# Cross attention: queries and keys in high and low parts, both projections on four 64x64 squares

## The chip, the core and the metric

The kernel runs on one core of a Trainium2 chip. The metric is the device time of one execution in microseconds (us). TensorE (PE) multiplies matrices, VectorE (DVE) and ScalarE (ACT) do the element-wise work, GpSimd (POOL) small side jobs, SyncE (SP) issues the DMAs. A matrix product has a part that is held in TensorE's array (the weights, loaded first: "PEld" in the profile) and a part that streams through it. The results land in PSUM, eight banks of 128 partitions x 512 floats.

## The reference, cut to what matters

One decoder layer on x (32 sequences of 64 tokens, 512 features): a linear attention with 32 heads, a cross attention, and a product with a 512x512 matrix. Each adds to x and starts with a layer norm. The change is in the cross attention, in the way its queries and keys are made and multiplied:

```python
q = jnp.einsum('dc,bct->btd', Wq, init) + bq
k = jnp.einsum('dc,bct->bdt', Wk, init) + bk[None, :, None]
R = jnp.einsum('btd,bds->bts', q, k)
attention = jax.nn.softmax(R, axis=-1)
v = jnp.einsum('oc,bct->bto', Wv, x) + bv
out = jnp.einsum('bts,bsc->bct', attention, v)
```

`init` is the context: 64 channels by 512 positions for each of 32 sequences. Wq and Wk are 64x64, so each sequence has a 64x512 query, a 64x512 key and 512x512 scores.

## The kernel before, in words

`attention` does the linear attention and is not touched. `cross_and_ffn` does the rest for pairs of sequences, t = 0 to 15; sequence 2t lies on partitions 0 to 63, sequence 2t+1 on 64 to 127. All engines run programs written out by hand, in order, joined by semaphores. Work on pair t is interleaved with the scores of pair t+1, the projections of pair t+2 and the last product (`ffn`) of pair t-1.

One pass of TensorE's loop over t is, in this order: `turn(t,0)` (8 transposes of probabilities), `project_q(t+2)`, `turn(t,1)`, `project_k(t+2)`, the scores of column blocks 0 and 1 of pair t+1, `spread_scale(t)`, `weigh(t,0)` and `weigh(t,1)` (probabilities times values), `turn(t,2)`, `values(t+1)`, the scores of blocks 2 and 3, `turn_xn3(t-1)`, `turn(t,3)`, `weigh(t,2)`, `weigh(t,3)`, `ffn(t-1)`. Passes 14 and 15 have no projection.

- `project_q` and `project_k` (L1177 to 1184) multiply 128 partitions of context by a 128x128 matrix that holds the 64x64 weight twice on its diagonal and zeros elsewhere. The operands are plain float32, and the trace has two matmul records for each such product.
- `cross_scores` (L1186 to 1193) takes one 64-row product for each sequence, held on rows 0 to 63 and 64 to 127 of the array, also in plain float32: two records each.
- ScalarE copies the projections out of PSUM with the bias (`keep_q`, `keep_k`). Both use bank 7 (MISC), one after the other; `spread_scale` and `values` use the same bank later.
- VectorE takes the maximum of each row of scores (`row_max`), ScalarE the exponentials (`exps`). Scores of blocks 0 and 2 go to banks 0 and 1, those of 1 and 3 to banks 2 and 3, so scores of block 3 wait for both exponentials of block 1.
- `ffn` already works with high and low parts: operands of type float32r, three products, one record each (L1249 to 1251).

Ahead of the loop, pair 0 is projected, scored and exponentiated, pair 1 projected, and the first two layer norms, `values(0)` and the high and low parts of the 512x512 matrix (`eye_hi`, `eye_lo`) are made.

Of the kernel before, what the change touches and what calls it, by code (L numbers as in the profile page):

```python
# [14 lines left out]
ACT = mybir.ActivationFunctionType  # L15
# [4 lines left out]
P = 128  # L20
# [27 lines left out]
class Prepared:  # L48


    def __init__(self, sb, sem, ctx_in, consts):
        self.ctx_in = ctx_in
        self.consts = consts
        self.ctx = sb("ctx", [P, 2, D])
        self.wq = sb("wq2", [P, P])
        self.wk = sb("wk2", [P, P])
        self.wv = sb("wv2", [P, P])
        self.bias = sb("bias2", [P, 3])
        self.ms = sb("ms", [P, TILES])
        self.ctx_landed = [sem(f"ctx_landed{i}") for i in range(2)]  # L60
        self.consts_landed = sem("consts_landed")
        self.summed = sem("summed")
        self.ms_ready = sem("ms_ready")
# [23 lines left out]

def load_ctx(sp, pre, t):
    sp.dma_start(pre.ctx[:, t % 2], pre.ctx_in[t]).then_inc(pre.ctx_landed[t % 2], 16)


def attention(nc, sb, sem, bank, attn_acc, sq_acc, ident, ones, pre, x, w_pairs, w_v, w_out, norm_w, decay, ident_in):
# [811 lines left out]
def cross_and_ffn(nc, sb, sem, bank, x1, ident, pre, x, eye_in, out):  # L904
    with ExitStack() as own:
        xr = sb(own, "xr", [P, TILES, D])
        rrms = sb(own, "rrms", [P, TILES])
        minus_half = sb(own, "minus_half2", [P, TILES])
        q = sb(own, "q", [P, 2, D])
        k = sb(own, "k", [P, 2, D])  # L910
        minus_max = sb(own, "minus_max", [P, 2, CH, 2])
        row_sum = sb(own, "row_sum", [P, 2, CH, 2])
        row_inv = sb(own, "row_inv", [P, 2, CH, 2])
# [14 lines left out]
        shift = sb(own, "shift", [P, 2])  # L928

        names = """rrms_ready x1_ready eye_landed consts_set eye_hi_cut eye_cut  # L930
            qk_mm qk_ready s_mm max_ready exp_ready inv_ready turned probT_a_ready probT_b_ready
            v_mm v_ready scale_mm scale_ready pv_mm scaled x2_ready
            ln2_stats ln2_var ln2_eps ln2_root ln2_rstd xn2_ready
            ln3_stats ln3_var ln3_eps ln3_root ln3_rstd xn3_ready
# [3 lines left out]
        x_t = x.rearrange("b s d -> (b s) d").rearrange("(k t p) d -> k p t d", t=TT, p=P)  # L938
        out_t = out.rearrange("b s d -> (b s) d").rearrange("(t p) d -> t p d", p=P)
        PAIRS = TILES  # L940
        PT, OUT, MISC = 4, 6, 7

        with nc.Block() as block:

            @block.sync
            def _(sp):
                def load_x(n):
                    sp.dma_start(xr[:, n * TT:(n + 1) * TT], x_t[n]).then_inc(x_back[n], 16)

                load_x(0)  # L950
                sp.dma_start(eye[:, :, :], eye_in).then_inc(S["eye_landed"], 16)
                for n in range(1, TB):
                    load_x(n)
                for t in range(PAIRS):
                    if t + 2 < PAIRS:
                        sp.wait_ge(S["qk_mm"], 2 * t + 2)
                        load_ctx(sp, pre, t + 2)
                    if t >= 2:
                        sp.wait_ge(S["out_ready"], t - 1)
                        sp.dma_start(out_t[t - 2], x1[:, t - 2]).then_inc(S["stored"], 16)  # L960
                for t in range(PAIRS - 2, PAIRS):
                    sp.wait_ge(S["out_ready"], t + 1)
                    sp.dma_start(out_t[t], x1[:, t]).then_inc(S["stored"], 16)
                sp.wait_ge(S["stored"], 16 * PAIRS)
# [28 lines left out]

            @block.scalar
            def _(act):
                def keep_q(t, at):
                    act.wait_ge(S["qk_mm"], 2 * t + 1)
                    nc.scalar.activation(q[:, t % 2], bank[:, at], ACT.Identity,
                                         bias=pre.bias[:, 0:1]).then_inc(S["qk_ready"], 1)

                def keep_k(t, at):
                    act.wait_ge(S["qk_mm"], 2 * t + 2)
                    nc.scalar.activation(k[:, t % 2], bank[:, at], ACT.Identity,
                                         bias=pre.bias[:, 1:2]).then_inc(S["qk_ready"], 1)

                def exps(t, j, i, at):
                    act.wait_ge(S["max_ready"], t * CH + (j + 1))
# [19 lines left out]
                    nc.scalar.activation(xn3_hi[:, :, :], bank[:, MISC].rearrange("p (c n) -> p c n", c=CH),  # L1027
                                         ACT.Copy).then_inc(S["xn3_hi_ready"], 1)

                keep_q(0, 6)  # L1030
                keep_k(0, 7)
                for j in range(CH):
                    for i in range(2):
                        exps(0, j, i, 2 * (j % 2))
                keep_q(1, 4)
                keep_k(1, 5)
                normed(2, 0, 0, xn2)
                act.wait_ge(S["v_mm"], 1)
                normed(2, 0, 1, xn2)
# [3 lines left out]
                for t in range(PAIRS):  # L1043
                    keep_turned(t, 0)
                    if t + 2 < PAIRS:
                        keep_q(t + 2, MISC)
                    keep_turned(t, 1)
                    if t + 2 < PAIRS:
                        keep_k(t + 2, MISC)
                    if t:  # L1050
                        normed(3, 1, t - 1, xn3)
                    if t + 1 < PAIRS:
                        exps(t + 1, 0, 0, 0)
                    keep_scale(t)
                    if t + 1 < PAIRS:
                        exps(t + 1, 0, 1, 0)
                        exps(t + 1, 1, 0, 2)
                    keep_turned(t, 2)
                    if t + 1 < PAIRS:
                        exps(t + 1, 1, 1, 2)  # L1060
                        exps(t + 1, 2, 0, 0)
                    if t:
                        xn3_high(t - 1)
                    keep_turned(t, 3)
                    if t + 1 < PAIRS:
                        exps(t + 1, 2, 1, 0)
                    if t + 1 < PAIRS:
                        exps(t + 1, 3, 0, 2)
                        exps(t + 1, 3, 1, 2)
                    if t + 2 < PAIRS:  # L1070
                        act.wait_ge(S["v_mm"], t + 2)
                        normed(2, 0, t + 2, xn2)
# [4 lines left out]
            def _(dve):  # L1077
                def row_max(t, j, at):
                    dve.wait_ge(S["s_mm"], t * CH + (j + 1))
                    nc.vector.tensor_reduce(minus_max[:, t % 2, j], bank[:, at:at + 2], AX.X, ALU.max,  # L1080
                                            negate=True).then_inc(S["max_ready"], 1)

                def inverse(t):
                    dve.wait_ge(S["exp_ready"], 2 * CH * (t + 1))
# [39 lines left out]
                def add_ffn(t):  # L1124
                    dve.wait_ge(S["ffn_mm"], t + 1)
                    nc.vector.tensor_tensor(x1[:, t], x1[:, t], bank[:, MISC], ALU.add).then_inc(S["out_ready"], 1)

                for j in range(CH):
                    row_max(0, j, 2 * (j % 2))
                dve.wait_ge(S["rrms_ready"], 1)  # L1130
                dve.wait_ge(x_back[0], 16)
                make_x1(0)
# [9 lines left out]
                                            ALU.subtract).then_inc(S["eye_cut"], 1)  # L1142
                for t in range(PAIRS):
                    keep_turned(t, 0)
                    keep_turned(t, 1)
                    if t + 1 < PAIRS:
                        row_max(t + 1, 0, 0)
# [26 lines left out]

            @block.tensor
            def _(pe):
                def project_q(t, at):  # L1177
                    pe.wait_ge(pre.ctx_landed[t % 2], 16 * (t // 2 + 1))
                    nc.tensor.matmul(bank[:, at], pre.wq[:, :], pre.ctx[:, t % 2], start=True, stop=True)\  # L1179
                        .then_inc(S["qk_mm"], 1)  # L1180

                def project_k(t, at):
                    nc.tensor.matmul(bank[:, at], pre.wk[:, :], pre.ctx[:, t % 2], start=True, stop=True)\  # L1183
                        .then_inc(S["qk_mm"], 1)

                def cross_scores(t, j, at):  # L1186
                    if j == 0:
                        pe.wait_ge(S["qk_ready"], 2 * t + 2)
                    for i in range(2):
                        s = slice(i * SEQ, (i + 1) * SEQ)  # L1190
                        m = nc.tensor.matmul(bank[:, at + i], q[s, t % 2, j * P:(j + 1) * P], k[s, t % 2],  # L1191
                                             start=True, stop=True)
                    m.then_inc(S["s_mm"], 1)

                def turn(t, c):
# [57 lines left out]
                    m.then_inc(S["ffn_mm"], 1)  # L1253

                pe.wait_ge(pre.consts_landed, 16 * 6)
                project_q(0, 6)
                project_k(0, 7)
                for j in range(CH):
                    if j == 2:
                        project_q(1, 4)  # L1260
                        project_k(1, 5)
                    if j >= 2:
                        pe.wait_ge(S["exp_ready"], 2 * (j - 1))
                    cross_scores(0, j, 2 * (j % 2))
                values(0)
                pe.wait_ge(S["qk_ready"], 4)
                pe.wait_ge(S["v_ready"], 1)
                for t in range(PAIRS):
                    turn(t, 0)
                    if t + 2 < PAIRS:  # L1270
                        if t >= 2:
                            pe.wait_ge(S["out_ready"], t - 1)
                        project_q(t + 2, MISC)
                    turn(t, 1)
                    if t + 2 < PAIRS:
                        pe.wait_ge(S["qk_ready"], 2 * t + 5)
                        project_k(t + 2, MISC)
                    if t + 1 < PAIRS:
                        cross_scores(t + 1, 0, 0)
                        cross_scores(t + 1, 1, 2)  # L1280
                    if t + 2 < PAIRS:
                        pe.wait_ge(S["qk_ready"], 2 * t + 6)
                    elif t >= 2:
                        pe.wait_ge(S["out_ready"], t - 1)
                    spread_scale(t)
# [74 lines left out]
```

## Time and profile before

| | us |
|---|---|
| three timed runs: median (lowest, highest) | 2226.3 (2224.16, 2227.65) |
| the profiled execution | 2226.27 |
| its span, first to last instruction | 2224.5 |
| PE busy, DVE busy, ACT busy | 2174.7, 1415.3, 1060.0 |
| linear attention, up to | 1896.5 |
| cross attention and last product | 328.0 |
| one pass of the loop over t | 18.68 |

Times in the rows below are microseconds from the start of the span. A timeline row has start, duration, engine, line, operation, output<-inputs, shapes and how many such instructions ran one after the other; in brackets stands how long the engine sat idle before and what ended that. A PE row's duration reaches to the modelled end of its last product, which overlaps the start of the next: the time that a group costs TensorE is the distance from its start to the start of the next group. On the array, "128*128" is the whole of it, "64*128" two halves by rows, "128*64" two halves by columns.

### The profile page before, as it was taken

The numbers are of one execution on the slowest core, as the hardware profiler recorded it, in microseconds if no ns is written. First come the engines' busy times: TensorE is split into PE (matmuls) and PEld (weight loads), VectorE is DVE, ScalarE is ACT, GpSimd is POOL, SyncE is SP. The second block draws the span as 40 slices with busy tenths as digits, with TensorE's granted clock in tenths as the row PEclk, the third lists the DMA queues.
The fourth block names the chain that finished last, engine by engine and source line by source line (L and its number), as shares of the span: only waits on it lengthen the run. The fifth ranks groups of instructions, "written<-read, shape, count | busy, mean of one in ns | idle before, by whom it ended". The sixth has DMA issues, their size and how long they took to land. (4 is left out here: it accounts for less than half of the span.)

```text
span 2224.5 us, 37071 instructions
## 1 busy us (share of the span) xinstructions
PE 2174.7 (98%) x13600; PEld 1793.2 (81%) x13600; DVE 1415.3 (64%) x1925; ACT 1060.0 (48%) x1799; POOL 651.9 (29%) x723
## 2 busy tenths in 40 slices
PE   6999999999999999999999999999999999799998
PEld 6888888888888888878888888888888888455555
DVE  6666666666666666676666666666666665577775
ACT  4444444444444444444444444444444443566664
POOL 5333333333333332343322333333333331111110
PEclk9999999999999999999999999999999999899999
DMA  3111111111111111111111111111111110200000
GB/s 128 57 49 41 47 40 48 48 48 48 48 48 48 48 40 47 50 39 41 48 48 48 48 48 48 48 40 46 41 48 48 48 49 23 110 29 29 29 24 20
DMA packets 37915, 104.91 MB, mean 47 GB/s; under 512 B 4448, under 2 KB 9056, under 8 KB 37728
## 3 DMA queue, kind: packets, MB, share of 16 engines
q1 hardware_dynamic: 37856, 104.10, 14.4%
q8 instruction: 39, 0.64, 0.1%
q14 instruction: 20, 0.16, 0.0%
HBM read 99.89 MB, written 4.19 MB: 47 GB/s over the span
## 5 line engine op out<-in xcount | busy, mean ns | idle before, releaser
L733 PE MATMUL bank<-x_hi,w_hi 128*128 128x512 f32 x1344 | 531.4, 395 | 2.4 <-ACT gate L384 2.4
L736 PE MATMUL bank<-x_hi,w_lo 128*128 128x512 f32 x1344 | 524.2, 390 | 1.2 <-issue 1.2
L735 PE MATMUL bank<-x_lo,w_hi 128*128 128x512 f32 x1344 | 523.1, 389 | 0.0
L733 PEld LDWEIGHTS bank<-x_hi,w_hi 128*128 128x128 f32 x1344 | 252.2, 188 | 59.3 <-ACT gate L384 3.3
L736 PEld LDWEIGHTS bank<-x_hi,w_lo 128*128 128x128 f32 x1344 | 252.3, 188 | 54.1
L735 PEld LDWEIGHTS bank<-x_lo,w_hi 128*128 128x128 f32 x1344 | 252.5, 188 | 50.8
L748 PE MATMUL bank<-wv_hi,x_hi 128*128 128x256 f32 x1024 | 293.1, 286 | 0.0
L306 POOL TENSOR_TENSOR sq_acc<-sq_acc,sq 128x512 f32<-128x512 f32 x124 | 160.5, 1295 | 445.7 <-ACT sq L434 432.5
L749 PE MATMUL bank<-wv_lo,x_hi 128*128 128x256 f32 x1024 | 290.4, 284 | 0.0
L750 PE MATMUL bank<-wv_hi,x_lo 128*128 128x256 f32 x1024 | 290.3, 283 | 0.0
L295 POOL TENSOR_TENSOR qk<-qk,sq 128x512 f32<-128x512 f32 x64 | 83.0, 1296 | 701.0 <-ACT sq L397 701.0
L506 DVE TENSOR_TENSOR w_lo<-raw,w_hi 128x1024 fp32r<-128x1024 f32 x192 | 239.5, 1249 | 8.8 <-ACT w_hi L349 8.8
L384 ACT ACTIVATE qk<-bank 128x512 f32<-128x512 f32 x192 | 115.2, 600 | 246.9 <-PE bank L736 246.6
L591 DVE TENSOR_TENSOR attn_acc<-attn_acc,bank 128x512 f32<-128x512 f32 x240 | 161.8, 685 | 69.9 <-PE bank L778 67.9
L776 PE MATMUL bank<-wo_hi,y_hi 128*128 128x512 f32 x512 | 203.3, 397 | 2.1 <-DVE y_lo L582 2.1
L778 PE MATMUL bank<-wo_hi,y_lo 128*128 128x512 f32 x512 | 202.6, 396 | 0.0
L777 PE MATMUL bank<-wo_lo,y_hi 128*128 128x512 f32 x512 | 202.5, 396 | 0.0
L349 ACT ACTIVATE w_hi<-raw 128x1024 fp32r<-128x1024 f32 x192 | 171.7, 945 | 57.5 <-POOL raw L282 57.5
L748 PEld LDWEIGHTS bank<-wv_hi,x_hi 128*128 128x128 f32 x1024 | 197.3, 193 | 1.2
L749 PEld LDWEIGHTS bank<-wv_lo,x_hi 128*128 128x128 f32 x1024 | 197.2, 193 | 1.2
L750 PEld LDWEIGHTS bank<-wv_hi,x_lo 128*128 128x128 f32 x1024 | 197.1, 193 | 0.0
L544 DVE TENSOR_TENSOR qk<-bank,qk 128x512 f32<-128x512 f32 x192 | 127.1, 689 | 85.2 <-ACT qk L399 42.7
(124 smaller groups left out, 3442.9 us busy)
## 6 DMA issues: line engine op xcount, KB each, us to landing
raw<-w_pairs SPq DMA_DIRECT2D x96, 512.0 KB, 3.4
raw<-w_v SPq DMA_DIRECT2D x32, 512.0 KB, 3.4
raw<-w_out SPq DMA_DIRECT2D x32, 512.0 KB, 3.3
ctx<-ctx_in SPq DMA_DIRECT2D x16, 256.0 KB, 2.8
xr<-x SPq DMA_DIRECT2D x4, 1024.0 KB, 10.9
out<-attn_acc SPq DMA_DIRECT2D x16, 256.0 KB, 2.0
attn_acc<-x SPq DMA_DIRECT2D x8, 256.0 KB, 6.5
decays<-decay SPq DMA_DIRECT2D x32, 64.0 KB, 1.9
```

The source lines that it names most:

```text
L349: nc.scalar.activation(dst[:, s], raw[:, s], ACT.Copy).then_inc(done, 1)
L506: nc.vector.tensor_tensor(dst[:, s], raw[:, s], hi[:, s].bitcast(F32), ALU.subtract).then_inc(done, 1)
L591: nc.vector.tensor_tensor(acc, acc, bank[:, out_bank(half, g, i)], ALU.add).then_inc(out_added, 1)
L733: nc.tensor.matmul(bank[:, to], w_hi[:, a, s], x_hi[:, b, c], start=part in ("first", "only") and c == 0, stop=False, skip_group_check=True)
L735: nc.tensor.matmul(bank[:, to], w_hi[:, a, s], x_lo[:, b, c], start=False, stop=False, skip_group_check=True)
L736: i = nc.tensor.matmul(bank[:, to], w_lo[:, a, s], x_hi[:, b, c], start=False, stop=part in ("last", "only") and c == 1, skip_group_check= ...
L748: nc.tensor.matmul(dst, x_hi[:, b, c % 2, s], wv_hi[:, m], start=(c == 0), stop=False)
L749: nc.tensor.matmul(dst, x_hi[:, b, c % 2, s], wv_lo[:, m], start=False, stop=False)
L750: k = nc.tensor.matmul(dst, x_lo[:, b, c % 2, s], wv_hi[:, m], start=False, stop=(c == CH - 1))
L776: nc.tensor.matmul(dst, y_hi[:, h, s], wo_hi[:, h], start=(h == 0), stop=False)
L777: nc.tensor.matmul(dst, y_hi[:, h, s], wo_lo[:, h], start=False, stop=False)
L778: k = nc.tensor.matmul(dst, y_lo[:, h, s], wo_hi[:, h], start=False, stop=(h == HG - 1))
```

## The change

Queries and keys are kept as two float32r numbers each, a high part (ScalarE's rounding copy) and a low part (what remains, a new operation of VectorE that reads PSUM and the high part). The scores are then the sum of three products, high x high, low x high and high x low, each on the same two 64-row halves of the array. Both projections of a pair are made by one function, as four 64x64 products, one in each quarter of the array: queries of the two sequences on the diagonal, keys on the other two. For the keys to land on the right partitions the context is also loaded with its halves swapped (`crossed`, two more DMAs for each pair). The second projection no longer has a place of its own in the loop; the keys get bank 3 (KEYS), which scores of block 1 need too, so these wait for the low part of the keys.

```diff
@@ load_ctx
     sp.dma_start(pre.ctx[:, t % 2], pre.ctx_in[t]).then_inc(pre.ctx_landed[t % 2], 16)
+    for i in range(2):
+        to, source = slice(i * SEQ, (i + 1) * SEQ), slice((1 - i) * SEQ, (2 - i) * SEQ)
+        sp.dma_start(pre.crossed[to, t % 2], pre.ctx_in[t, source]).then_inc(pre.ctx_landed[t % 2], 16)
@@ ScalarE
-                    nc.scalar.activation(k[:, t % 2], bank[:, at], ACT.Identity,
-                                         bias=pre.bias[:, 1:2]).then_inc(S["qk_ready"], 1)
+                def k_high(t, at):
+                    act.wait_ge(S["qk_mm"], t + 1)
+                    nc.scalar.activation(k_hi[:, t % 2], bank[:, at], ACT.Identity,
+                                         bias=pre.bias[:, 1:2]).then_inc(S["k_hi_ready"], 1)
                     keep_turned(t, 0)
                     if t + 2 < PAIRS:
-                        keep_q(t + 2, MISC)
+                        k_high(t + 2, KEYS)
+                        q_high(t + 2, MISC)
                     keep_turned(t, 1)
-                    if t + 2 < PAIRS:
-                        keep_k(t + 2, MISC)
@@ VectorE
+                def k_low(t, at):
+                    dve.wait_ge(S["k_hi_ready"], t + 1)
+                    nc.vector.scalar_tensor_tensor(out=k_lo[:, t % 2], in0=bank[:, at], scalar=pre.bias[:, 1:2],
+                                                   in1=k_hi[:, t % 2].bitcast(F32), op0=ALU.add, op1=ALU.subtract)\
+                        .then_inc(S["k_ready"], 1)
+                k_low(0, 7)
+                q_low(0, 6)
                 for j in range(CH):
                     row_max(0, j, 2 * (j % 2))
+                k_low(1, 5)
+                q_low(1, 4)
                 dve.wait_ge(S["rrms_ready"], 1)
                 dve.wait_ge(x_back[0], 16)
                 make_x1(0)
...
                     keep_turned(t, 0)
+                    if t + 2 < PAIRS:
+                        k_low(t + 2, KEYS)
+                        q_low(t + 2, MISC)
                     keep_turned(t, 1)
@@ TensorE
+                def project_qk(t, at_q, at_k):
+                    pe.wait_ge(pre.ctx_landed[t % 2], 48 * (t // 2 + 1))
+                    for r in range(2):
+                        rows, other = slice(r * SEQ, (r + 1) * SEQ), slice((1 - r) * SEQ, (2 - r) * SEQ)
+                        nc.tensor.matmul(bank[rows, at_q], pre.wq[rows, rows], pre.ctx[rows, t % 2], start=True, stop=True)
+                        m = nc.tensor.matmul(bank[other, at_k], pre.wk[rows, rows], pre.crossed[rows, t % 2],
+                                             start=True, stop=True)
+                    m.then_inc(S["qk_mm"], 1)
...
-                    for i in range(2):
-                        s = slice(i * SEQ, (i + 1) * SEQ)
-                        m = nc.tensor.matmul(bank[:, at + i], q[s, t % 2, j * P:(j + 1) * P], k[s, t % 2],
-                                             start=True, stop=True)
+                    for n, (a, b) in enumerate(((q_hi, k_hi), (q_lo, k_hi), (q_hi, k_lo))):
+                        for i in range(2):
+                            s = slice(i * SEQ, (i + 1) * SEQ)
+                            m = nc.tensor.matmul(bank[:, at + i], a[s, t % 2, j * P:(j + 1) * P], b[s, t % 2],
+                                                 start=(n == 0), stop=(n == 2))
...
                     turn(t, 0)
                     if t + 2 < PAIRS:
                         if t >= 2:
                             pe.wait_ge(S["out_ready"], t - 1)
-                        project_q(t + 2, MISC)
+                        project_qk(t + 2, MISC, KEYS)
                     turn(t, 1)
-                    if t + 2 < PAIRS:
-                        pe.wait_ge(S["qk_ready"], 2 * t + 5)
-                        project_k(t + 2, MISC)
                     if t + 1 < PAIRS:
                         cross_scores(t + 1, 0, 0)
+                        if t + 2 < PAIRS:
+                            pe.wait_ge(S["k_ready"], t + 3)
                         cross_scores(t + 1, 1, 2)
                     if t + 2 < PAIRS:
-                        pe.wait_ge(S["qk_ready"], 2 * t + 6)
+                        pe.wait_ge(S["q_ready"], t + 3)
```

`q_high` and `q_low` are the same for the queries.

How this moves TensorE's instructions, in the loop from one `ffn` to `values`. Before (L1203 is `turn`, L1179 and L1183 the projections, L1191 the scores, L1232 `spread_scale`, L1216 `weigh`, L1225 `values`):

```order
L1251 MATMUL bank<-eye_hi,xn_lo 128x512
L1203 MATMUL bank<-ident,prob 128x128 x8
L1179 MATMUL bank<-ctx,wq 128x512
L1203 MATMUL bank<-ident,prob 128x128 x8
L1183 MATMUL bank<-ctx,wk 128x512
L1191 MATMUL bank<-k,q 128x512 x4
L1232 MATMUL bank<-ident,row_inv 64x128 x8
L1216 MATMUL bank<-probT,v 64x512 x4
L1203 MATMUL bank<-ident,prob 128x128 x8
L1225 MATMUL bank<-wv,xn 128x128 x4
```

The same place in the changed kernel (L1230 is `turn`, L1206 and L1207 the squares, L1218 the scores, L1259 `spread_scale`):

```order
L1230 MATMUL bank<-ident,prob 128x128 x8
L1206 MATMUL bank<-ctx,wq 64x512
L1207 MATMUL bank<-crossed,wk 64x512
L1206 MATMUL bank<-ctx,wq 64x512
L1207 MATMUL bank<-crossed,wk 64x512
L1230 MATMUL bank<-ident,prob 128x128 x8
L1218 MATMUL bank<-k_hi,q_hi 128x512 x2
L1218 MATMUL bank<-k_hi,q_lo 128x512 x2
L1218 MATMUL bank<-k_lo,q_hi 128x512 x2
L1218 MATMUL bank<-k_hi,q_hi 128x512 x2
L1218 MATMUL bank<-k_hi,q_lo 128x512 x2
L1218 MATMUL bank<-k_lo,q_hi 128x512 x2
```

The key projection has moved from behind the second `turn` to the side of the query projection, and two blocks of scores are twelve products where they were four.

VectorE in the loop, from `add_ffn` to the first layer norm, before (L1126 is `add_ffn`, L1089 the copies of `turn`, L1080 `row_max`, L1092 `make_x1`):

```order
L1126 TENSOR_TENSOR attn_acc<-attn_acc,bank 128x512
L1089 COPY probT<-bank 128x512 x2
L1080 TENSOR_REDUCE minus_max<-bank 128x2 x2
L1092 SCALAR_TENSOR_TENSOR attn_acc<-attn_acc,rrms,xr 128x512
L1098 BN_STATS stats<-attn_acc 128x6
```

And in the changed kernel:

```order
L1143 TENSOR_TENSOR attn_acc<-attn_acc,bank 128x512
L1106 COPY probT<-bank 128x512
L1096 SCALAR_TENSOR_TENSOR k_lo<-bank,bias,k_hi 128x512
L1090 SCALAR_TENSOR_TENSOR q_lo<-bank,bias,q_hi 128x512
L1106 COPY probT<-bank 128x512
L1085 TENSOR_REDUCE minus_max<-bank 128x2 x2
L1109 SCALAR_TENSOR_TENSOR attn_acc<-attn_acc,rrms,xr 128x512
L1115 BN_STATS stats<-attn_acc 128x6
```

The two new operations stand between the copies of `turn(t,0)` and `turn(t,1)`, and so ahead of the maxima that the exponentials of pair t+1 wait for.

## Rows read from the trace of the kernel before

**Rows 1.** Windows: us, PE, PEld, DVE, ACT, POOL busy (instructions), PEclk, DMA share, GB/s
```profile
1910.80:1924.40 13.60, 8.50 (x28) 5.98 (x28) 5.36 (x9) 5.71 (x10) 1.94 (x6) 0.50 0.15 59
1924.40:2180.00 255.60, 254.06 (x1476) 145.87 (x1475) 182.17 (x259) 160.44 (x359) 28.37 (x81) 1.00 0.08 26
```
**Rows 2.** Timeline of PE, one pass of the loop (t = 9)
```profile
2087.24 1.03 PE L1203 MATMUL bank<-ident,prob 128*128 128x128 f32 x8
2088.18 1.13 PE L1179 MATMUL bank<-ctx,wq 128*128 128x512 f32 x2
...
2090.09 1.12 PE L1183 MATMUL bank<-ctx,wk 128*128 128x512 f32 x2
2091.14 1.99 PE L1191 MATMUL bank<-k,q 64*128 64x512 f32 x8
2093.06 1.09 PE L1232 MATMUL bank<-ident,row_inv 128*64 128x128 f32 x16
2093.98 1.89 PE L1216 MATMUL bank<-probT,v 128*64 128x512 f32 x8
...
2097.72 1.99 PE L1191 MATMUL bank<-k,q 64*128 64x512 f32 x8
...
2103.85 0.40 PE L1249 MATMUL bank<-eye_hi,xn_hi 128*128 128x512 f32 x1
2104.08 0.39 PE L1250 MATMUL bank<-eye_lo,xn_hi 128*128 128x512 f32 x1
...
2105.92 1.03 PE L1203 MATMUL bank<-ident,prob 128*128 128x128 f32 x8
```
**Rows 3.** Timeline of PEld, same pass: loads of the first scores and weights
```profile
2091.14 0.30 PEld L1191 LDWEIGHTS bank<-k,q 64*128 64x128 f32 x4 [0.76 <-issue]
...
2093.88 0.25 PEld L1216 LDWEIGHTS bank<-probT,v 128*64 128x64 f32 x4
```
**Rows 4.** Timeline of PE, pass 14, which has no projection
```profile
2182.56 1.07 PE L1203 MATMUL bank<-ident,prob 128*128 128x128 f32 x8 [0.87 <-DVE probT L1089]
2183.55 0.70 PE L1191 MATMUL bank<-k,q 64*128 64x512 f32 x2
```
**Rows 5.** Timeline of ACT, pass t = 9
```profile
2089.35 0.69 ACT L998 ACTIVATE q<-bank,bias 128x512 f32<-128x512 f32 x1 [0.43 <-PE bank L1179]
...
2093.58 0.69 ACT L1008 ACTIVATE prob<-bank,minus_max 128x512 f32<-128x512 f32 x1 [0.94 <-DVE minus_max L1080]
...
2095.97 0.22 ACT L1008 ACTIVATION_READ_ACCUMULATOR prob<-bank,minus_max 128x1 f32 x1
2096.93 0.60 ACT L1014 ACTIVATE probT<-bank 128x512 f32<-128x512 f32 x1 [0.75 <-PE bank L1203]
2097.42 0.68 ACT L1008 ACTIVATE prob<-bank,minus_max 128x512 f32<-128x512 f32 x1
2097.99 0.20 ACT L1008 ACTIVATION_READ_ACCUMULATOR prob<-bank,minus_max 128x1 f32 x1
```
**Rows 6.** Timeline of DVE, same pass
```profile
2088.31 0.69 DVE L1089 COPY probT<-bank 128x512 f32<-128x512 f32 x1 [0.19 <-PE bank L1203]
...
2092.32 2.35 DVE L1080 TENSOR_REDUCE minus_max<-bank 128x2 f32<-128x1024 f32 x2 [1.37 <-PE bank L1191]
```
**Rows 7.** Timeline ahead of the loop and in its pass 0, ACT
```profile
1910.35 0.69 ACT L1003 ACTIVATE k<-bank,bias 128x512 f32<-128x512 f32 x1
...
1917.71 2.19 ACT L1042 ACTIVATE eye_hi<-eye 128x512 fp32r<-128x512 f32 x4 [1.75 <-issue]
```
**Rows 8.** The same stretch, DVE
```profile
1908.32 0.74 DVE L1092 SCALAR_TENSOR_TENSOR attn_acc<-attn_acc,rrms,xr 128x512 f32<-128x512 f32 x1
```
**Rows 9.** The same stretch, PE
```profile
1921.62 1.94 PE L1203 MATMUL bank<-ident,prob 128*128 128x128 f32 x8 [2.30 <-DVE probT L1089]
1923.35 1.56 PE L1183 MATMUL bank<-ctx,wk 128*128 128x512 f32 x2
1924.84 1.99 PE L1191 MATMUL bank<-k,q 64*128 64x512 f32 x8
```

More of the change, by code:

```diff
@@ L54, in __init__ @@
         self.ctx = sb("ctx", [P, 2, D])
+        self.crossed = sb("crossed", [P, 2, D])
         self.wq = sb("wq2", [P, P])
@@ L908, in cross_and_ffn @@
         minus_half = sb(own, "minus_half2", [P, TILES])
-        q = sb(own, "q", [P, 2, D])
-        k = sb(own, "k", [P, 2, D])
+        q_hi = sb(own, "q_hi", [P, 2, D], F32R)
+        q_lo = sb(own, "q_lo", [P, 2, D], F32R)
+        k_hi = sb(own, "k_hi", [P, 2, D], F32R)
+        k_lo = sb(own, "k_lo", [P, 2, D], F32R)
         minus_max = sb(own, "minus_max", [P, 2, CH, 2])
@@ L930, in cross_and_ffn @@
         names = """rrms_ready x1_ready eye_landed consts_set eye_hi_cut eye_cut
-            qk_mm qk_ready s_mm max_ready exp_ready inv_ready turned probT_a_ready probT_b_ready
+            qk_mm q_hi_ready k_hi_ready q_ready k_ready s_mm max_ready exp_ready inv_ready turned probT_a_ready probT_b_ready
             v_mm v_ready scale_mm scale_ready pv_mm scaled x2_ready
@@ L940, in cross_and_ffn @@
         PAIRS = TILES
-        PT, OUT, MISC = 4, 6, 7
+        KEYS, PT, OUT, MISC = 3, 4, 6, 7
         with nc.Block() as block:
@@ L955, in _ @@
                     if t + 2 < PAIRS:
-                        sp.wait_ge(S["qk_mm"], 2 * t + 2)
+                        sp.wait_ge(S["qk_mm"], t + 1)
                         load_ctx(sp, pre, t + 2)
@@ L995, in _, with q_high @@
             def _(act):
[L996 to L1002, printed above, removed]
-                    nc.scalar.activation(k[:, t % 2], bank[:, at], ACT.Identity,
-                                         bias=pre.bias[:, 1:2]).then_inc(S["qk_ready"], 1)
+                def q_high(t, at):
+                    act.wait_ge(S["qk_mm"], t + 1)
+                    nc.scalar.activation(q_hi[:, t % 2], bank[:, at], ACT.Identity,
+                                         bias=pre.bias[:, 0:1]).then_inc(S["q_hi_ready"], 1)
+                def k_high(t, at):
+                    act.wait_ge(S["qk_mm"], t + 1)
+                    nc.scalar.activation(k_hi[:, t % 2], bank[:, at], ACT.Identity,
+                                         bias=pre.bias[:, 1:2]).then_inc(S["k_hi_ready"], 1)
                 def exps(t, j, i, at):
@@ L1028, in xn3_high @@
                                          ACT.Copy).then_inc(S["xn3_hi_ready"], 1)
-                keep_q(0, 6)
-                keep_k(0, 7)
+                k_high(0, 7)
+                q_high(0, 6)
                 for j in range(CH):
@@ L1034, in _ @@
                         exps(0, j, i, 2 * (j % 2))
-                keep_q(1, 4)
-                keep_k(1, 5)
+                k_high(1, 5)
+                q_high(1, 4)
                 normed(2, 0, 0, xn2)
@@ L1081, in row_max, with q_low @@
                                             negate=True).then_inc(S["max_ready"], 1)
+                def q_low(t, at):
+                    dve.wait_ge(S["q_hi_ready"], t + 1)
+                    nc.vector.scalar_tensor_tensor(out=q_lo[:, t % 2], in0=bank[:, at], scalar=pre.bias[:, 0:1],
+                                                   in1=q_hi[:, t % 2].bitcast(F32), op0=ALU.add, op1=ALU.subtract)\
+                        .then_inc(S["q_ready"], 1)
+                def k_low(t, at):
[3 more added lines that the diff above has]
+                        .then_inc(S["k_ready"], 1)
                 def inverse(t):
@@ L1176, in _ @@
             def _(pe):
[L1177 to L1184, printed above, removed]
+                def project_qk(t, at_q, at_k):
[6 more added lines that the diff above has]
+                    m.then_inc(S["qk_mm"], 1)
                 def cross_scores(t, j, at):
                     if j == 0:
-                        pe.wait_ge(S["qk_ready"], 2 * t + 2)
-                    for i in range(2):
-                        s = slice(i * SEQ, (i + 1) * SEQ)
-                        m = nc.tensor.matmul(bank[:, at + i], q[s, t % 2, j * P:(j + 1) * P], k[s, t % 2],
-                                             start=True, stop=True)
+                        pe.wait_ge(S["q_ready"], t + 1)
+                        pe.wait_ge(S["k_ready"], t + 1)
+                    for n, (a, b) in enumerate(((q_hi, k_hi), (q_lo, k_hi), (q_hi, k_lo))):
[3 more added lines that the diff above has]
+                                                 start=(n == 0), stop=(n == 2))
                     m.then_inc(S["s_mm"], 1)
@@ L1255, in _ @@
                 pe.wait_ge(pre.consts_landed, 16 * 6)
-                project_q(0, 6)
-                project_k(0, 7)
+                project_qk(0, 6, 7)
                 for j in range(CH):
                     if j == 2:
-                        project_q(1, 4)
-                        project_k(1, 5)
+                        project_qk(1, 4, 5)
                     if j >= 2:
@@ L1265, in _ @@
                 values(0)
-                pe.wait_ge(S["qk_ready"], 4)
+                pe.wait_ge(S["q_ready"], 2)
+                pe.wait_ge(S["k_ready"], 2)
                 pe.wait_ge(S["v_ready"], 1)
```

## The prediction

> **What bounds the kernel now.** I read the windows first, then the timelines of one pass of the loop over t, then the stretch ahead of the loop. The change leaves all up to 1896.5 us alone, so it can only act on the 328 us behind. From 1924.4 to 2180.0 PE is busy 254.1 of 255.6 us at a granted clock of 1.00, DVE 182.2, ACT 160.4 [rows 1]. A busy PE is not yet a PE that nothing holds up, so the timeline has to say it: in the pass from 2087.24 to 2105.92 (18.68 us) each group starts before the modelled end of the one before it [rows 2]. So TensorE's order sets the pass, and what leaves its order counts in full until something else is late. DVE works some 13.3 of the 18.68 us of a pass (182.2 of 255.6), ACT 11.7; they have room, but not at any moment.
>
> Ahead of the loop it is otherwise: TensorE waits 2.30 us for DVE at 1921.62 [rows 9], and from 1910.8 to 1924.4 the granted clock is 0.50, that is 1.2 GHz, with PE busy in 8.5 of 13.6 us [rows 1].
>
> **The change part by part.** The sum is made against the profiled execution, 2226.27 us (span 2224.5 and 1.8 around it); the median shown is 2226.3, the same for this purpose. I count times in a pass from its first row, 2087.24.
>
> *Projections.* From `project_q` at 2088.18 to the scores at 2091.14 lie 2.96 us: query projection, `turn(t,1)`, key projection [rows 2]. Afterwards there is one slot of squares and `turn(t,1)`. Pass 14, without projection, shows `turn(t,1)` directly ahead of the scores: 0.99 from start to start [rows 4]. For the slot of the squares I take 1.05, what `project_k` costs when the array's division changes behind it [rows 2]: all four squares stream 512 columns twice, as it does, if they run side by side. 2.96 - 1.05 - 0.99 = 0.92 saved in a pass. That they run side by side is the first thing no row shows. Nearest are `weigh`, two products in column halves that share all rows: 8 records end within 1.89 us and the first four weight loads take 0.25 [rows 2, 3], so they run in twos at 0.43 each (8 single ones at 0.43 would take 3.4); and the scores, two in row halves: 8 records in 1.92 [rows 2]. Squares are both at once. Bounds: four at once, and two at once, 0.86 more. I take four, since both halvings work.
>
> *Scores.* Two blocks cost 1.92 now: 8 records in twos, 4 x 0.43, and 0.20 of change of division. A block is 0.86. Products of float32r operands start 0.23 apart in `ffn` (2103.85 to 2104.08) [rows 2]. Three passes in twos: 0.69 a block, 0.17 less, four blocks 0.68 in a pass. Their weight loads: four 64-row loads fit in 0.30, in twos [rows 3], and one pair is needed every 0.23. Bounds: 0.43 / 2 for each pair, 0.65 a block, and, if these products don't run in twos, 6 x 0.23 = 1.38.
>
> *VectorE.* `k_low` and `q_low` are scalar_tensor_tensor of 128x512; this operation takes 0.74 on SBUF [rows 8]. Bounds 0.69 (a copy out of PSUM) and 1.22 (one `row_max` over twice the elements; two take 2.35) [rows 6]. I take 0.74, the nearest in kind. 13.3 + 1.5 = 14.8 us of a pass of over 17: no bound by volume. But they stand ahead of the maxima, so the chain behind them is to be walked. Squares start at 0.94; their copy starts 1.17 later as `q`'s does [rows 5], 2.11; `k_high` 0.69, 2.80; `k_low` to 3.57; `q_high` is ready by 3.5, `q_low` to 4.31; the copy of `turn(t,1)` to 5.00; first maximum 1.22, 6.22; first exponential at 6.26. Before it was at 2093.58, 6.34. So the two operations fit into the 1.37 us for which DVE waits now, nearly to the last tenth [rows 6]. The waits for `k_low` ahead of block 1 (3.57, PE comes there at 3.0 + 0.7 = 3.7) and for `q_low` ahead of `spread_scale` (4.31, PE comes at 4.6) cost nothing.
>
> *The wait that appears.* Scores of block 3 need both exponentials of block 1. From the first exponential to the third's readout are 2.61 us (2093.58 to 2096.19), the copy of `turn(t,2)` takes 0.49 of ACT (2096.93 to 2097.42), the fourth with readout 0.77 (to 2098.19) [rows 5]: 6.26 + 2.61 + 0.49 + 0.77 = 10.13, and 0.1 to TensorE, 10.23. Now that copy waits for TensorE and block 3 is reached at 2097.72 + 0.86, 11.34 [rows 2]. Afterwards TensorE comes at 11.34 - 0.92 - 3 x 0.17 = 9.91 and waits 0.32. Behind the waiting product stand `turn_xn3`, `turn(t,3)`, `weigh` and `ffn`, so the whole pass shifts.
>
> A pass: 0.92 + 0.68 - 0.32 = 1.28 less, 17.4 instead of 18.68. Passes 1 to 13: 16.6. Pass 14 has only the scores, 0.6. Pass 0 behind its first scores: 0.68 less the same wait, 0.3.
>
> *Ahead of the loop.* `make_x1(0)` starts at 1908.32, when the maxima are done [rows 8]. Now `k_low(1)` and `q_low(1)` stand before it, and need ACT's copies of pair 1, which stand behind all eight exponentials: the second of them starts at 1910.35 [rows 7]. Half a microsecond earlier, for the quicker first scores, it ends at 1910.5; two low parts of 0.74, from 1910.0 on, end at 1911.5. `make_x1(0)` is 3.2 us later, and with it the layer norm, `values(0)`, `eye_hi`, `eye_lo`, and the copy of `turn(0,0)` that TensorE waits for at 1921.62 [rows 9]. ACT's pause of 1.75 ahead of `eye_hi` has no engine that ends it [rows 7]. Does it move along, all is 3.2 late; does it end at the same moment, 1.4. I take the first: `turn(0,1)` at 1924.8, 1.73 for it at the half clock (1921.62 to 1923.35), and the scores at 1926.4 instead of 1924.84 [rows 9], since `project_k` is gone there too. Loss 1.5; bounds 0 (pause hidden) and 3.4 (the clock, at 0.50 for that stretch, rises later).
>
> *DMAs.* Two more issues a pass on SP, which issues two now (a context and a result), and nobody waits on its queue in a pass; a context is used a whole pass after its issue. Nothing.
>
> *Sum.* 16.6 + 0.6 + 0.3 - 1.5 = 16.0, so 2226.3 - 16.0 = 2210.3.
>
> *Division of the array.* The step from scores to `spread_scale` shows what a change costs: 1.92 less 4 x 0.43 is 0.20 [rows 2]. The squares add one change ahead and one behind. The Trainium skill (TensorEngine Tiling (Array Packing), Key Properties) says that changing the tiling mode drains TensorE. By it I would charge both at 0.20 where the sum holds 0.19 for both (1.05 less 0.86): 0.2 more a pass, 2.7 us, 2213. The trace agrees that a change costs, not that each costs 0.20: `turn` to scores is 0.99 where `turn` to `project_q` is 0.94 [rows 2, 4].
>
> **The rivals.** The *squares run two at a time*. Two squares share each 64 rows. For: no row has quarters. Against: `weigh`'s halves share all rows and run together. Slot 0.86 longer, and the chain of exponentials too, so the wait stays 0.32: 0.92 - 0.86 + 0.68 - 0.32 = 0.42 a pass, 5.5; 0.9 for passes 0 and 14; 1.5 lost ahead and 1.7 for the slot at half clock in pass 0: 2223. The Trainium skill (TensorE: Matmul & The Clock Gate, Part 3, The mechanism) has a rule that leads here: a weight load overlaps running products only if its row group is another. `weigh`'s four loads in 0.25 us speak against it.
>
> *Weight loads set the pace of the scores.* Each pair of 64-row products needs two loads of 128 columns; if the four loads' 0.30 is the price of one pair, a block costs 0.90. For: the loads are the only thing that comes more often, 6 a block instead of 4. Against: in twos they are hidden now. 0.92 - 0.16 = 0.76 a pass and no wait (TensorE comes at 10.5): 9.9 - 0.2 - 1.5 = 8.2, 2218.
>
> *Low parts are slow*, 1.22 each: the chain is 0.96 longer, the wait 1.28, 0.32 a pass: 4.2 + 0.9 - 2.5, 2224.
>
> *The other side: float32r halves don't run together.* The three passes add six products a block to TensorE, each 0.23 if single: 1.38, 0.52 more than now. It decides from 0.86 + 0.92 / 4 = 1.09 a block. Passes 1 to 13: 13 x (2.08 - 0.92) = 15.1, passes 0 and 14 4.2, ahead 1.5: 2247. For: all float32r products of this trace use the whole array, every half is plain float32. Against: float32's own records run in twos, and the division belongs to the array.
>
> **How the numbers follow.** Forecast 0.60, squares in twos 0.13, loads set the pace 0.12, slow low parts 0.05, halves not together 0.08, something else 0.02. 0.2% is 4.5 us, about what a measurement of this kernel tells from no change: faster means below 2221.8, slower above 2230.8. Forecast, the loads' case and a third of the next two: 0.78 faster. The rest of these two 0.12 the same, 0.10 slower. The likeliest case alone spans 2206 (block 0.65, nothing lost ahead, no wait) to 2216 (3.4 lost, wait doubled). For 8 in 10 the range is 2204 to 2225; it leaves out the case of single halves.
>
> **What would show it.** Right: 17.4 us from `turn(t,0)` to `turn(t+1,0)`; about 1.05 from squares to `turn(t,1)` with eight records in twos of 0.43; two blocks of scores in 1.58; a wait of some 0.3 of TensorE for ACT's exponentials ahead of block 3; `make_x1(0)` near 1911.5. Wrong: a slot of squares of 1.9, score products 0.23 apart one by one, `k_low` over 1 us, or an ordinary pass above 18 us.

## The result

| | before | changed |
|---|---|---|
| median of the timed runs, us | 2225.23 (4 runs) | 2207.44 (4 runs) |
| the profiled execution / its span | 2226.27 / 2224.5 | 2205.04 / 2203.2 |
| one pass of the loop over t | 18.68 | 17.20 |

The ratio is 0.9922, with a 95% interval of 0.9903 to 0.9942: 0.8% faster. Two more comparisons of the same two kernels gave 0.9916 (0.9903 to 0.9928) and 0.9922 (0.9907 to 0.9936). Forecast were 2210.3 us and 17.4 us a pass.

One pass of TensorE, t = 9 as in [rows 2]; a timeline's columns are those named there:

```profile
2074.83 1.03 PE L1230 MATMUL bank<-ident,prob 128*128 128x128 f32 x8
2075.79 0.64 PE L1206 MATMUL bank<-ctx,wq 64*64 64x512 f32 x1
2075.80 0.64 PE L1207 MATMUL bank<-crossed,wk 64*64 64x512 f32 x1
2075.80 0.64 PE L1206 MATMUL bank<-ctx,wq 64*64 64x512 f32 x1
2075.81 0.64 PE L1207 MATMUL bank<-crossed,wk 64*64 64x512 f32 x1
2076.27 0.59 PE L1206 MATMUL bank<-ctx,wq 64*64 64x512 f32 x1
...
2076.81 1.09 PE L1230 MATMUL bank<-ident,prob 128*128 128x128 f32 x8
2077.83 0.50 PE L1218 MATMUL bank<-k_hi,q_hi 64*128 64x512 f32 x2
2078.17 0.39 PE L1218 MATMUL bank<-k_hi,q_lo 64*128 64x512 f32 x2
2078.40 0.39 PE L1218 MATMUL bank<-k_lo,q_hi 64*128 64x512 f32 x2
...
2079.42 1.09 PE L1259 MATMUL bank<-ident,row_inv 128*64 128x128 f32 x16
...
2084.07 0.50 PE L1218 MATMUL bank<-k_hi,q_hi 64*128 64x512 f32 x2
...
2084.88 0.40 PE L1218 MATMUL bank<-k_hi,q_hi 64*128 64x512 f32 x2
...
2085.68 0.66 PE L1268 MATMUL bank<-ident,xn 128*128 128x128 f32 x4
...
2092.03 1.03 PE L1230 MATMUL bank<-ident,prob 128*128 128x128 f32 x8
```

Four squares start within 0.02 us of each other, their second records 0.48 later, all four again together: the slot costs 1.02. Score products start in twos, the second pair 0.34 after the first, the others 0.23 to 0.24 apart, and two blocks take 1.59 and 1.61. Nothing waits between blocks 2 and 3.

Where the 21.3 us between the two profiled spans lie, from starts in both timelines:

| stretch | before | changed | difference | forecast |
|---|---|---|---|---|
| up to the first projection | 1896.65 | 1893.84 | -2.8 | 0 |
| from there to the scores (1,0) of pass 0 | 28.19 | 29.88 | +1.7 | +1.5 |
| from there to pass 1 | 12.98 | 13.50 | +0.5 | -0.3 |
| passes 1 to 13 | 242.82 | 223.61 | -19.2 | -16.6 |
| pass 14 | 17.68 | 17.10 | -0.6 | -0.6 |
| pass 15 to the end | 26.18 | 25.27 | -0.9 | 0 |

The first and the last stretch hold the same work in both kernels. Over all profiles taken, the first projection starts anywhere from 1893.8 to 1898.4 us, at 1893.8 and 1896.6 for one and the same (the changed) kernel, and the last stretch takes 25.2 to 26.2 for it. So nothing shows that these 3.7 us belong to the change. The timed difference of 17.8 us fits the four stretches between (17.6).

### The profile page after: what moved, and what is told of

Same layout as the page of the kernel before. It is cut to its first block and busy times, and to the rows that moved or that the text cites. A ratio compares the mean times of both kernels' runs of the same rounds, so it can differ in the third digit from the quotient of the medians.

```text
span 2203.2 us, 37536 instructions
## 1 busy us (share of the span) xinstructions
PE 2150.2 (98%) x13792; PEld 1799.1 (82%) x13792; DVE 1433.7 (65%) x1957; ACT 1054.8 (48%) x1799; POOL 651.0 (30%) x723
```

## The experiments

Pass lengths below are from the first transposes of one pass to those of the next, from pass 2 to pass 14. Within a kernel they agree to 0.05 us, so one profile is enough for them.

**The squares alone.** Scores back in plain float32, no low parts; squares, slot and bank as in the change.

```diff
-                    for n, (a, b) in enumerate(((q_hi, k_hi), (q_lo, k_hi), (q_hi, k_lo))):
+                    for n, (a, b) in enumerate(((q_hi, k_hi),)):
                         for i in range(2):
...
-                k_low(1, 5)
-                q_low(1, 4)
...
-                        k_low(t + 2, KEYS)
-                        q_low(t + 2, MISC)
```

(`q_hi` and `k_hi` are then float32 and release the scores themselves.)

> Squares and the merged slot kept, scores back to plain float32 products, no high and low parts, no low-part work on VectorE. If TensorE's order sets the pass: two blocks of scores cost 1.92 again instead of 1.59, twice a pass, 17.20 + 0.66 = 17.86 us a pass, some 9 us more than the changed kernel over 14 passes. If the chain of maxima and exponentials set the pass of 17.20, the three operations taken off VectorE and ScalarE would give part of it back: under 17.7.

Ratio 0.9950 (0.9931 to 0.9968), median 2211.53 us against 2225.44, 17.78 a pass. Its pass, TensorE:

```profile
2078.42 1.09 PE L1223 MATMUL bank<-ident,prob 128*128 128x128 f32 x8
2079.44 1.99 PE L1211 MATMUL bank<-k_hi,q_hi 64*128 64x512 f32 x8
2081.36 1.09 PE L1252 MATMUL bank<-ident,row_inv 128*64 128x128 f32 x16
```

Two blocks cost 1.92 again. The squares and the slot are worth 18.68 - 17.78 = 0.90 a pass (0.92 counted), the three products for one on top 0.58 (0.68 counted). The blocks themselves give 0.64 (0.33 and 0.31); the rest is lost at `weigh(t,2)` and `weigh(t,3)`, which take 2.01 us here (2087.14 to 2089.15), 1.96 before and in this run. From the first projection to `values(0)` are 16.07 us, as before (16.11), where the changed kernel has 19.71: the later start belongs to the low parts.

**The parts alone.** High and low parts kept, projections on the whole array, each in its old place, both in bank 7.

```diff
-                        project_qk(t + 2, MISC, KEYS)
+                        project_q(t + 2, MISC)
                     turn(t, 1)
+                    if t + 2 < PAIRS:
+                        pe.wait_ge(S["q_ready"], t + 3)
+                        project_k(t + 2, MISC)
```

> High and low parts and three passes kept; projections back to two products on the whole array, in their old places and both in bank 7, without the crossed context. If each part of the change were worth its TensorE time alone: 18.68 - 0.66 = 18.0. If the low part, which reads bank 7, holds up the second projection: query low part ready at 3.67 of the pass where the key projection could start at 2.85, so 0.8 waited there, the scores of block 3 not held up, 18.9 a pass, not faster than the kernel before.

Ratio 1.0028 (1.0018 to 1.0037), median 2230.25 us, 18.93 a pass: slower than before. Its pass:

```profile
2075.22 1.13 PE L1206 MATMUL bank<-ctx,wk 128*128 128x512 f32 x2 [0.66 <-DVE q_lo L1088]
2076.27 0.51 PE L1224 MATMUL bank<-k_hi,q_hi 64*128 64x512 f32 x2
```

The key projection waits for VectorE's `q_lo`, which reads bank 7: it starts 1.73 us after `turn(t,1)` (from 2073.49), where 0.94 lie between them before the change (2089.15 to 2090.09). That is 0.79 lost, against 0.61 that the four blocks of scores give; with 0.07 more at `weigh` it makes up the 0.25 a pass by which this version is slower. So the two parts of the change don't add up one by one: three products alone lose 0.25 a pass, and on top of the merged slot, with the keys in a bank of their own, they gain 0.58.

**Two whole-array products in the slot of the squares.**

```diff
-                    for r in range(2):
-                        ...
+                    nc.tensor.matmul(bank[:, at_q], pre.wq[:, :], pre.ctx[:, t % 2], start=True, stop=True)
+                    m = nc.tensor.matmul(bank[:, at_k], pre.wk[:, :], pre.ctx[:, t % 2], start=True, stop=True)
```

> As the changed kernel, but in the slot of the squares stand two products on the whole array (diagonal weights), and no crossed context is loaded. If four squares really run together: the slot costs 1.88 instead of 1.02, the chain of exponentials moves by as much, 17.20 + 0.86 = 18.06 a pass. If the gain was that of the merged slot and not of the squares: 17.2.

18.00 a pass, one time of 2213.30 us. Its slot:

```profile
2081.57 1.13 PE L1201 MATMUL bank<-ctx,wq 128*128 128x512 f32 x2
2082.53 1.02 PE L1202 MATMUL bank<-ctx,wk 128*128 128x512 f32 x2
2083.39 1.04 PE L1224 MATMUL bank<-ident,prob 128*128 128x128 f32 x8
```

1.82 instead of 1.02. The squares by themselves are worth 0.80 a pass, and the pass is longer by just what the slot is. Squares that run in twos had been priced at 0.86 more for the slot, nearly this.

**Half by half.** The loops over i and n in `cross_scores` exchanged, so that the three products of rows 0 to 63 are issued before the three of rows 64 to 127.

```diff
-                    for n, (a, b) in enumerate(((q_hi, k_hi), (q_lo, k_hi), (q_hi, k_lo))):
-                        for i in range(2):
+                    for i in range(2):
+                        for n, (a, b) in enumerate(((q_hi, k_hi), (q_lo, k_hi), (q_hi, k_lo))):
```

> As the changed kernel, but the three products of one half of the array are issued before the three of the other, instead of in turn. If products start strictly in the order issued, the halves overlap only at the seam: 0.92 a block instead of 0.69, 17.20 + 4 x 0.23 = 18.1 a pass. If each half has its own queue, nothing changes: 17.2.

17.22 a pass, one time of 2205.84 us: no difference. Its block:

```profile
2078.62 0.50 PE L1218 MATMUL bank<-k_hi,q_hi 64*128 64x512 f32 x2
2078.95 0.40 PE L1218 MATMUL bank<-k_hi,q_lo 64*128 64x512 f32 x2
2079.18 0.40 PE L1218 MATMUL bank<-k_lo,q_hi 64*128 64x512 f32 x2
```

The first products of both halves still start together (a row `x2` holds one product of each half), though two others of the first half stand between them in the program. In this run each half takes its products as from a queue of its own. This is against a sentence of the Trainium skill (TensorE: Matmul & The Clock Gate, Part 3, The mechanism), that products start in strict program order; here the measurement decides.

**No low parts.** The three products all take the high parts (the low terms are left out of the scores), VectorE makes none.

```diff
-                    for n, (a, b) in enumerate(((q_hi, k_hi), (q_lo, k_hi), (q_hi, k_lo))):
+                    for n, (a, b) in enumerate(((q_hi, k_hi), (q_hi, k_hi), (q_hi, k_hi))):
...
-                        k_low(t + 2, KEYS)
-                        q_low(t + 2, MISC)
```

> As the changed kernel with no low parts made: the three products all take the high parts, so the result lacks the low ones; TensorE's work is the same, VectorE has 1.34 us less a pass and the chain to the exponentials is shorter. If TensorE alone sets the pass: 17.20, unchanged. If VectorE's chain sets it: about 16.9.

One time of 2205.02 us; two passes begin at

```profile
2074.84 1.03 PE L1223 MATMUL bank<-ident,prob 128*128 128x128 f32 x8
...
2092.04 1.03 PE L1223 MATMUL bank<-ident,prob 128*128 128x128 f32 x8
```

17.20, unchanged. In the loop, the 1.32 us that the low parts take of VectorE in a pass (2077.67 to 2078.99 in the changed kernel) cost nothing; TensorE's order sets the pass.

**Low parts twice.** In the loop, each made once more into a spare tile ahead of the real one.

```diff
                 def k_low(t, at, times=1):
                     dve.wait_ge(S["k_hi_ready"], t + 1)
+                    if times == 2:
+                        nc.vector.scalar_tensor_tensor(out=spare[:, 1], in0=bank[:, at], scalar=pre.bias[:, 1:2],
+                                                       in1=k_hi[:, t % 2].bitcast(F32), op0=ALU.add, op1=ALU.subtract)
```

> As the changed kernel, each low part in the loop made twice (the first into a spare tile). The two more operations start 0.67 apart, so the chain to the exponentials is 1.33 longer. It ends 0.1 ahead of TensorE now, by the trace, so TensorE should wait 1.2 at the scores of block 3 and the pass be 18.4. If the chain has more room than that: under 18.0; if VectorE's volume binds: no other number, 16.2 of 18.4 busy.

18.33 a pass, one time of 2222.16 us: nearly the length expected, but most of the wait not at the place expected. TensorE, from one block to the next:

```profile
2089.04 0.39 PE L1225 MATMUL bank<-k_lo,q_hi 64*128 64x512 f32 x2
2089.77 0.50 PE L1225 MATMUL bank<-k_hi,q_hi 64*128 64x512 f32 x2 [0.34 <-DVE k_lo L1103]
...
2091.09 1.09 PE L1266 MATMUL bank<-ident,row_inv 128*64 128x128 f32 x16 [0.35 <-DVE q_lo L1094]
...
2096.31 0.40 PE L1225 MATMUL bank<-k_lo,q_hi 64*128 64x512 f32 x2
2096.61 0.19 PEld L1225 LDWEIGHTS bank<-k_hi,q_hi 64*128 64x128 f32 x2 [0.34 <-ACT prob L1015]
2096.61 0.50 PE L1225 MATMUL bank<-k_hi,q_hi 64*128 64x512 f32 x2
```

TensorE is 0.50 late at block 1 (2089.04 to 2089.77, where 0.23 is usual) and 0.53 at `spread_scale` (1.32 after block 1, where 0.79 is usual), both times for a low part. At block 3 it is late by less than 0.1 only, this time for the fourth exponential. 1.32 of work more, 1.13 of pass more.

How much room each of the three waits has in the changed kernel can be read from the two traces. In this run TensorE starts 0.06 after the end of what it waits for, at all three places. In the changed kernel it starts 0.21 after `k_lo` has ended (2078.42 to 2078.63), 0.34 after `q_lo` (2079.08 to 2079.42) and 0.28 after the fourth readout (2084.60 to 2084.88). So the room is 0.15 at block 1, 0.28 at `spread_scale` and 0.22 at block 3. The last one bounds the pass: 1.32 - 0.22 = 1.10 more, by estimate, whether TensorE has waited earlier in the pass or not. The two direct waits took up 1.03 of it before block 3 was reached.

**The norm first.** Ahead of the loop, VectorE makes `make_x1(0)`, the layer norm and `make_x1(1)` before the low parts of pair 1.

```diff
-                k_low(1, 5)
-                q_low(1, 4)
                 dve.wait_ge(S["rrms_ready"], 1)
                 dve.wait_ge(x_back[0], 16)
                 make_x1(0)
                 layernorm(2, 0, 0)
                 inverse(0)
                 make_x1(1)
+                k_low(1, 5)
+                q_low(1, 4)
```

> As the changed kernel, but ahead of the loop VectorE makes x1 and the layer norm of tile 0 (and x1 of tile 1) before the low parts of pair 1, which nobody needs before pass 0's scores. If those two operations are what delayed the start: values(0) 3.5 us earlier, and 2 to 3.5 us less in all, 0.1 to 0.15 per cent. If the stretch is bound by the input load or code fetch: no difference.

> The changed kernel itself, beside the others on the same chip, for the comparison with the norm-first version: 0.992 of the kernel before, 17.20 a pass.

Ratio 0.9909 (0.9896 to 0.9922) against 0.9916 (0.9903 to 0.9928) of the change, medians 2204.43 and 2204.57. In the trace the stretch is shorter: from the first projection to `values(0)` 15.91 us instead of 19.47, to pass 2 56.66 instead of 60.18. Both were run again, side by side:

> The norm-first version again. Its trace had 3.5 us less between the first projection and pass 2 than the changed kernel's, and its time was the same, since the linear attention, whose code is the same, took 3.3 us longer in that execution. If that was chance: the stretch from the first projection to pass 2 is again 56.7 and the median is 1 to 3.5 us below the changed kernel's. If the two go together: the same time again, with the first projection near 1897.

> The changed kernel beside it: 60.2 us from the first projection to pass 2, 17.20 a pass, first projection near 1894 if the linear attention's time belongs to the kernel, anywhere from 1894 to 1898 if it is chance.

Ratios 0.9901 (0.9887 to 0.9915) and 0.9922 (0.9907 to 0.9936), medians 2202.04 and 2206.79; to pass 2 58.36 and 61.81. So the stretch is 3.4 to 3.5 us shorter in both pairs. In time the version was ahead twice, by 0.1 and 4.8 us of medians, and the intervals overlap: it is at least as fast as the change and the fastest that was run, but how much of the 3.5 us reaches the end is open. The first projection of the norm-first version came at 1897.13 and 1898.42, that of the change at 1893.83 and 1896.58: 3.3 and 1.8 later, against 3.5 gained behind it. Two profiles of each don't tell whether this is chance.

## Why the prediction was right

**What bounds the kernel.** TensorE's order, before and after. The runs show it for the changed kernel: with less work on VectorE the pass stays 17.20, and with 0.80 more in TensorE's slot of squares it is 0.80 longer.

**The sum.** It came within 1.8 us because its misses partly cancel. The wait, counted at 0.32 a pass, did not come (4.2 us over passes 1 to 13). The savings of TensorE were counted at 1.60 a pass and are 1.48 (1.6 us the other way). Pass 0 came out 0.8 us worse than forecast and the stretch ahead of it 0.2. That makes 16.0 + 4.2 - 1.6 - 0.8 - 0.2 = 17.6.

**Projections**, 0.92 a pass: measured 0.90, with the squares four at once and at 1.02 instead of 1.05. The rival of squares in twos fell: all four start within 0.02 us, so the two that share 64 rows do too, and so do their loads. Of the loads of the first and of the second records:

```profile
2075.79 0.13 PEld L1206 LDWEIGHTS bank<-ctx,wq 64*64 64x64 f32 x1 [0.17 <-DVE attn_acc L1143]
2075.80 0.13 PEld L1207 LDWEIGHTS bank<-crossed,wk 64*64 64x64 f32 x1
...
2075.84 0.13 PEld L1206 LDWEIGHTS bank<-ctx,wq 64*64 64x64 f32 x1
```

The Trainium skill has the rule behind this rival (TensorE: Matmul & The Clock Gate, Part 3, The mechanism): a weight load overlaps running products only if its row group is another. The trace does not agree: the second four loads start at 2075.84 to 2075.86, while the first products of all four squares run.

**Scores**, 0.68 a pass: 0.33 + 0.31 measured at the blocks, 0.58 of the pass. The pace is that of `ffn` [rows 2], 0.23, halves together; neither single halves nor the loads set another. `turn` to the scores takes 1.02 [rows 4: 0.99], and two blocks still hold some 0.2 beyond six pairs at 0.23.

**VectorE's low parts**, 0.74 each: 0.75 and 0.74. But the sum of the chain took whole durations, and operations on VectorE start before the one ahead has ended. Of the changed kernel, DVE and then ACT:

```profile
2077.67 0.75 DVE L1096 SCALAR_TENSOR_TENSOR k_lo<-bank,bias,k_hi 128x512 fp32r<-128x512 f32 x1 [1.08 <-ACT k_hi L1009]
2078.34 0.74 DVE L1090 SCALAR_TENSOR_TENSOR q_lo<-bank,bias,q_hi 128x512 fp32r<-128x512 f32 x1
2078.99 0.68 DVE L1106 COPY probT<-bank 128x512 f32<-128x512 f32 x1
2079.59 2.35 DVE L1085 TENSOR_REDUCE minus_max<-bank 128x2 f32<-128x1024 f32 x2
```

```profile
2080.84 0.69 ACT L1014 ACTIVATE prob<-bank,minus_max 128x512 f32<-128x512 f32 x1 [1.44 <-DVE minus_max L1085]
...
2084.37 0.23 ACT L1014 ACTIVATION_READ_ACCUMULATOR prob<-bank,minus_max 128x1 f32 x1
```

From `k_low` to the maxima are 1.92 us where 2.17 were counted (0.67, 0.65 and 0.60 from start to start for 0.74, 0.74 and 0.69). The first exponential is at 6.01 of the pass instead of 6.26. From there to the fourth readout are 3.76 instead of 3.87, because ScalarE's copy starts at 2083.32, before the third readout has ended (2083.44). So the fourth is read out at 9.77 instead of 10.13. TensorE comes to block 3 at 10.05 instead of 9.91: block 2 takes 0.81 until block 3 starts, where 0.69 was counted.

**The wait that appears**, 0.32 a pass: this is the step that was wrong. It measures nothing; block 3 has 0.22 of room instead. Of these 0.54 us, 0.25 come from VectorE's operations counted by their durations, 0.11 from ScalarE's, 0.14 from TensorE reaching block 3 later, and 0.04 from the release, 0.06 us and not 0.1. Passes 1 to 13 are 19.2 shorter instead of 16.6. The chain to the exponentials was still rightly looked at: doubling the low parts shows that its room bounds the pass. The room at the two direct waits was read rightly, 0.1 and 0.3 for a measured 0.15 and 0.28.

**Ahead of the loop**, 1.5: measured 1.7, and in part by luck. The prediction's own terms give 1.7: 1924.8 and 1.73 make 1926.5, not 1926.4. `make_x1(0)` is 3.6 us later where 3.2 were forecast, seen from the first projection: 11.67 before, 15.30 after [rows 8].

```profile
1909.14 0.74 DVE L1109 SCALAR_TENSOR_TENSOR attn_acc<-attn_acc,rrms,xr 128x512 f32<-128x512 f32 x1
```

ACT's pause ahead of `eye_hi` moved along, 1.71 us long, as had been chosen:

```profile
1918.45 2.19 ACT L1048 ACTIVATE eye_hi<-eye 128x512 fp32r<-128x512 f32 x4 [1.71 <-issue]
```

`turn(0,1)` then starts 3.55 later (28.52 after the first projection instead of 24.97), and takes 1.36 to the scores where 1.73 was counted. The granted clock, forecast at 0.50 throughout, was 1.00 from 1920.1 to 1922.3, while TensorE stood idle, and 0.50 again from 1923.0 on. In two other profiles of the changed kernel this `turn` takes 1.87, and the stretch from the first projection to these scores is 29.93 and 30.30 instead of 29.88.

**Pass 0**, 0.3 gained: 0.5 lost. The first scores of the pass ran at the half clock (granted 0.50 from 1923.7 to 1926.1), their products 0.42 apart, where before they fell just behind the return to the full one at 1924.4 [rows 1, 9]. The prediction had named a clock that rises later as a bound of the stretch ahead, but kept it out of pass 0:

```profile
1924.32 0.63 PE L1218 MATMUL bank<-k_hi,q_lo 64*128 64x512 f32 x2
1924.74 0.63 PE L1218 MATMUL bank<-k_lo,q_hi 64*128 64x512 f32 x2
```

Two blocks at half rate cost about 1.2 more (2.76 from 1923.72 to 1926.48, against 1.59). How much of this is lost differs from execution to execution: in two other profiles of the changed kernel these two blocks take 2.26 and 2.86.

**DMAs**, nothing: SP issues four a pass, `crossed` among them, and no engine waited for a context.

## What to carry to other kernels

When an engine's own order sets the pace, price a change by the starts of its groups, and price the chain that could take over by start-to-start distances too, not by durations: 0.36 us too much in this chain was the larger part of what made a wait of 0.3 out of a room of 0.2. Ask of each new wait by itself how much room it has; doubling the suspected operation shows it, and the start after the end of what is waited for tells the size. Two parts of a change can need each other: the three cheaper products cost time here until the key projection, which waited for a low part, had a bank of its own.

## What was not expected of the hardware

- Four 64x64 squares, float32, run at once: 1.02 us for all, about what the one whole-array key projection took before (1.05 [rows 2]), where two whole-array products take 1.82.
- Two halves of the array by rows don't wait for each other's order. Products issued three and three still run in twos (17.22 a pass against 17.20).
- TensorE's granted clock was 1.00 from 1920.1 to 1922.3, with TensorE idle, between stretches at 0.50. How much of pass 0 then runs at 0.50 differs between executions of the changed kernel (its first two blocks take 2.26, 2.76 and 2.86 us).
- The linear attention, the same code each time, ended, by the start of the first projection, between 1893.8 and 1898.4 us. Profiles should be compared from a mark behind it.
